# A selective scan fused with its decoder layer: the last chunk's production four pairs earlier, the out-projection in three pieces a tile

## The reference, cut to what matters

```python
xz = x @ W_in + b_in                                # 512 -> 2 x 1024
x_proj, z = jnp.split(xz, 2, axis=-1)
x_conv = silu(x_proj)                               # u
B, C = jnp.split(x_conv @ W_xproj + b_xproj, 2, axis=-1)        # 16 states each
dt = softplus(x_conv @ W_dt + b_dt)                 # 1024 -> 1024
# per token: h = h * exp(dt * A) + (dt * u) * B ; y = sum_s(h * C) + D * u
y = selective_scan(x_conv, dt, A, B, C, D_param)
y = y * silu(z)
x = layernorm(x + y @ W_out + b_out)
```

## Time and profile before

| | us |
|---|---|
| median of 3 runs | 3091.01 |
| lowest, highest | 3089.64, 3095.03 |
| the profiled execution | 3090.05 |
| its span | 3088.3 |
| scan phase: first scan, end of last scan | 57.2, 1916.9 |
| TensorE busy in the span | 2836.5 (92%) |
| VectorE busy | 2700.7 (87%) |
| ScalarE busy | 2008.9 (65%) |
| GpSimd busy | 1822.1 (59%) |

### The profile page before, as it was taken

One profiled execution on the slowest core, in us unless ns is written; L12 is line 12 of the kernel. 1 busy time (PEld: TensorE's weight loads), 2 busy tenths in 40 slices (PEclk: granted clock), 3 DMA queues, 4 the chain that ended last, 5 costly groups with the idle time before them and its releaser, 6 DMA issues. The chain is left out here.

```text
span 3088.3 us, 49028 instructions
## 1 busy us (share of the span) xinstructions
PE 2836.5 (92%) x18958; PEld 1265.0 (41%) x18958; DVE 2700.7 (87%) x3074; ACT 2008.9 (65%) x3598; POOL 1822.1 (59%) x936
## 2 busy tenths in 40 slices
PE   7988989889889889889899898999999999999998
PEld 2222222222222222222222223566666767667765
DVE  6999999999999999999999988776766777777775
ACT  6777777776776776776777644555555565655565
POOL 4887988988888888888988887312211111111100
PEclk9999999999999999999999999999999999999999
DMA  4112121111121121121112233701111000010000
GB/s 163 52 52 70 38 66 56 52 60 51 49 65 53 42 66 53 41 65 53 46 61 80 88 97 121 230 30 43 43 45 47 29 23 23 23 37 29 23 8 15
DMA packets 123897, 176.65 MB, mean 57 GB/s; under 512 B 15154, under 2 KB 50610, under 8 KB 123156
## 3 DMA queue, kind: packets, MB, share of 16 engines
q1 hardware_dynamic: 123668, 173.51, 17.4%
HBM read 104.33 MB, written 67.04 MB: 55 GB/s over the span
## 5 line engine op out<-in xcount | busy, mean ns | idle before, releaser
L900 POOL TENSOR_TENSOR h<-h,c_rep 128x1024 f32<-128x1024 f32 x511 | 1198.3, 2361 | 238.0 <-ACT carry L652 236.9
L796 DVE TENSOR_TENSOR_SCAN h<-r_ps,carry,h 128x512 f32<-128x512 f32 x768 | 949.2, 1289 | 3.6 <-ACT r_ps L646 3.6
L646 ACT ACTIVATE r_ps<-r_ps,decay 128x512 f32<-128x512 f32 x1024 | 632.7, 657 | 319.7 <-PE r_ps L397 318.9
L783 DVE TENSOR_TENSOR h<-u_ps,b_rep 128x1024 f32<-128x1024 f32 x512 | 625.8, 1222 | 10.8 <-PE u_ps L410 10.6
L410 PE MATMUL u_ps<-dtu,spread 32*128 32x512 f16 x2048 | 312.9, 383 | 117.3 <-DVE h L783 115.8
L397 PE MATMUL r_ps<-dt,spread 32*128 32x512 f16 x2048 | 313.1, 382 | 44.6 <-DVE h L796 44.4
L1979 POOL TENSOR_TENSOR o_in<-o_in,rows 128x1024 f32<-128x1024 f32 x15 | 37.0, 2469 | 489.0 <-DMA o_in<-o_dram 489.0
L796 DVE TENSOR_TENSOR_SCAN h<-r_ps,zero,h 128x512 f32<-128x512 f32 x256 | 315.1, 1278 | 7.1 <-ACT r_ps L646 7.0
L426 PE MATMUL y_ps<-h,gather 128*32 128x512 f32 x2048 | 284.8, 623 | 0.0
L40 PE MATMUL fps<-x,region 128*128 128x256 f16 x1024 | 280.3, 274 | 3.1 <-issue 2.4
L41 PE MATMUL fps<-x,region 128*128 128x256 f16 x1024 | 279.9, 273 | 0.0
(11 more groups left out here) (257 smaller groups left out, 5602.4 us busy)
## 6 DMA issues: line engine op xcount, KB each, us to landing
u_t_dram<-u SPq DMA_DIRECT2D x16, 1024.0 KB, 5.3
uz<-u_t_dram SPq DMA_DIRECT2D x64, 256.0 KB, 3.9
z_t_dram<-zs SPq DMA_DIRECT2D x32, 512.0 KB, 2.8
uz<-z_t_dram SPq DMA_DIRECT2D x64, 256.0 KB, 3.9
y_t_dram<-uz SPq DMA_DIRECT2D x64, 256.0 KB, 2.1
region<-y_t_dram SPq DMA_DIRECT2D x32, 256.0 KB, 3.5
result<-x SPq DMA_DIRECT2D x16, 512.0 KB, 2.8
x_t<-dram_x_t SPq DMA_DIRECT2D x15, 512.0 KB, 5.0
```

Of the source, the lines that this page charges most:

```text
L646: nc.scalar.activation(bank, bank, ACT.Exp, scale=decay[:, col:col + 1]).then_inc(s_da, 1)
L783: nc.vector.tensor_tensor(h[:, g % H_GROUPS, o:o + 2, :], u_ps[:, :, :], b_rep[:, c % 2:c % 2 + 1, :].broadcast_to([P, 2, TS]), ALU.mult). ...
L796: nc.vector.tensor_tensor_scan(row, r_ps[:, 2 * (pair % 2) + o, :], row, start, ALU.mult, ALU.add)\
L900: nc.gpsimd.tensor_tensor(rows, rows, c_rep[:, c % 2:c % 2 + 1, :].broadcast_to([P, 2, TS]), ALU.mult)\
```

## The change

The plan of chunk 7 starts at pair 22 of chunk 6 instead of 26, so that dt7 ends at s = 16 instead of 20; its x halves are converted at 15 and 20 instead of 19 and 23. Chunk 6's plan has no four-pair dt tiles any more (it ends at pair 20 of chunk 6 instead of 25). `w_out` is split from pair 11 (ScalarE) and 13 (VectorE). The out-projection starts at 19; first pieces stand at 19, 22, 25, 28, 31, 33, 36, 39, 42, 45, 47, 50, 53, 56, 59, 61; each tile has three pieces but tiles 4, 9, 14 and 15, which have two; the last piece is at 62. `x0_tile` runs a pair later, behind the scans of the pair after the tile's last. `keep_awake` covers two pairs (17, 18) instead of three. Some of SyncE's stores and loads in chunks 6 and 7 move up in its list.

```diff
-W_OUT_AT, OUT_AT = 15, 24
+W_OUT_AT, OUT_AT = 11, 19
...
-        start = {1: 32, 2: 27}.get(n, 26)
-        self.x = {1: (25, 28), 2: (21, 24)}.get(n, (19, 23))
+        start = {1: 32, 2: 27, NC - 1: 22}.get(n, 26)
+        self.x = {1: (25, 28), 2: (21, 24), NC - 1: (15, 20)}.get(n, (19, 23))
...
-            long = name in ("dt4", "dt5", "dt6", "dt7") and 2 <= n < NC - 1 or name == "dt3" and 3 <= n < NC - 1
+            long = name in ("dt4", "dt5", "dt6", "dt7") and 2 <= n < NC - 2 or name == "dt3" and 3 <= n < NC - 2
...
 class OutTile:
     def __init__(self, i):
-        at = OUT_AT + i // 2 * 5 + i % 2 * 3
-        self.pieces = {at + n: ks for n, ks in enumerate(((0, 4), (4, NJ)) if i % 2 else ((0, 3), (3, 6), (6, NJ)))}
+        at = OUT_AT + 3 * i - i // 5
+        self.pieces = {at + n: ks for n, ks in enumerate(((0, 4), (4, NJ)) if i % 5 == 4 or i == OUT_TILES - 1
+                                                         else ((0, 3), (3, 6), (6, NJ)))}
...
-                if j == 1:
+                if j == (1 if more else 0):
                     store_z(c, 2)
-                if j == 2:
+                if j == (2 if more else 1):
                     store_z(c, 3)
+                if j == 2 and c == NC - 2:
+                    next_x(c + 1, 1)
+                if j == 7 and c == NC - 2:
+                    store_z(c + 1, 1)
...
-                    if j == 2:
+                    if j == 2 and c < NC - 2:
                         next_x(c + 1, 1)
...
-                    if j == 7:
+                    if j == 7 and c < NC - 2:
                         store_z(c + 1, 1)
...
-                if s == OUTS[0].last:
+                if s == OUTS[0].last + 1:
                     x0_tile(0)
-                if s == OUTS[1].last:
+                if s == OUTS[1].last + 1:
                     x0_tile(1)
                     dve.wait_ge(s_oe, 2)
                     dve.sem_inc(a["s_x0"], 1)
```

## The result

| | before | after |
|---|---|---|
| median (20 runs of each) | 3093.45 | 3102.01 |
| lowest, highest | 3088.24, 3098.10 | 3096.43, 3104.77 |
| ratio, 95% interval | | 1.0027 [1.0021, 1.0033] |
| profiled execution | 3090.05 | 3100.17 |
| its span | 3088.3 | 3098.5 |

The account below looks back on a forecast made before the run. VectorE was taken to bound the scan phase. Terms -0.5 (chunk 6), 6.3 + 1.2 - 8.41 (out-projection's start), 2.9 + 0.8 - 5.17 (later pieces) and -2.0 (end) gave -4.9 from 3090.05: 3085.2, median 3085.5, range 3081 to 3089.5.

Parts of the forecast that it names:

- Part 1: Production four pairs sooner, chunk 6: VectorE covers the denser TensorE pairs; -0.5 us, idle of 1.22 could vanish or double.
- part 3: Out-projection's start in chunk 7: 6.3 us of waits plus 1.2 for the clock replace 8.41 idle.
- hold by tile 1's landing: Start of the out-projection: ScalarE held 5.3 us at y_high(1) by tile 1's late y, delaying exps(23); VectorE idles 3.6.
- Tile 1's pieces: Out-projection's start: pieces behind y_low(1, 0) and y_low(1, 1) cost VectorE 2.05 us, then two waits of 0.5 and 0.15.
- The clock: TensorE spells at the lower clock in chunk 7: 1.2 us added at the out-projection's start, 0.8 later; bounds 0 and 6.8.
- third rival: Long lower-clock spells after TensorE's waits at 19 and 21, up to 5.1 us each; say 3098, slower; chance 0.08.
- Part 4: Three pieces a tile, chunk 7 from pair 28: 2.9 us of late pieces plus 0.8 clock replace 5.17 idle.
- its four pairs: Chunk 7 pairs s = 31, 33, 47 and 61, said to pass 5.85 us and idle together 2.9.
- Part 5: End of the scan phase: last piece at 62 frees the carry, last gate sooner; gain 2.0 us, bounds 0 and 3.3.
- Part 2: w_out split from pair 11 in chunk 7: the same 7.5 us of VectorE work four pairs sooner, 0 change.
- second rival: Denser production makes TensorE late in 9-matmul pairs of chunks 5 to 7, giving back 3.8 us: 3089; chance 0.10.

Follow-up runs that it names:

- e3: Kernel after, with chunk 7's second x half converted at pair 19 instead of 20 and chunk 6's dt6 and dt7 splits later; 3092.36 us against before's 3091.61.
- e6: e3, with SyncE loading b_out, x and tile 1's y ahead of the weights and the wait for dt7; 3089.97 us, 0.9990 of before.
- e2: Kernel before, with only x0_tile a pair later; 3086.76 us against before's 3091.61.
- e10: e3, with the out-projection from pair 21, two-piece tiles where i % 3 == 2, and w_out split from pair 15; 3085.84 us against before's 3093.05.
- e11: e10, with w_out split from pair 11 instead of 15; 3086.69 us, 0.9978 of before.
- e8: Kernel before, with x0_tile a pair later, e6's loads first and chunk 7's dt6 and dt7 splits later; 3087.35 us against before's 3092.36.
- e5: e3, with chunk 7's dt6 and dt7 splits also moved later, to pairs 22 and 26; 3091.04 us, 0.9992 of before.
- e7: e3, with both e5's late splits and e6's loads first; 3094.36 us, 0.9993 of before.
- e12: e3, with the out-projection in its old places (15, 24) and x0_tile a pair later; 3093.31 us against before's 3093.05.

## Why the prediction was wrong

**Part 1 failed, and it carries the sign.** It looked at TensorE, pair by pair, and found cover: that was right (e3 keeps every matmul where it is and has no stop). The step that failed is "SyncE's moved stores and x load wait for conversions that also come four pairs sooner; I find none that holds back a load of u or z for a following tile: 0". It asked of the conversions only what the loads want of them. Nobody counted GpSimd, whose work of chunk 6's dt tiles (now denser) and of chunk 7's x (now sooner) falls into the same pairs: 30.4 us in 24.9, with the x half that u0's second piece waits for at their end. The term was -0.5; measured +9.0, outside its bounds of +-1.2. The row to read would have been GpSimd's busy time: 199.27 of 229.00 leaves 30 us in 64 pairs, half a us a pair.

**The start of the out-projection (part 3) failed by one missing waiter.** "TensorE waits 3.6 us" was worked out, and then priced only where `exps(23)` are late. Behind the waiting piece stand the sums of s = 19, and the gate of s = 20 waits for them. By the forecast's own numbers the piece starts at 11.1, its 9 matmuls take 2.0 and the sums 1.07, so the gate could start at 14.2, 1.3 later than the 12.9 (1755.53 - 1742.64) at which VectorE was free. To that come 2.4 (dt7 ended on GpSimd at 12.3 instead of 9.9, after TensorE's spell at the lower clock; in e3, without the long spell, it ended as foreseen) and 1.9 (the 9 matmuls and sums took 5.0 us at the lower clock, not 3.1). 1.3 + 2.4 + 1.9 = 5.6 of 5.66. The hold by tile 1's landing was 1.68 instead of 5.3, since the gate's stop hides the landing, and e6 shows that nothing is won without it. Tile 1's pieces cost 1.80 and 1.63 where 2.05 and 0.65 were foreseen. Together s = 16 to 26 idle 10.1, with the clock, against 7.5 foreseen and 8.41 before.

**The clock was undersized, the mechanism was there.** The first out piece and the first piece behind the stop in chunk 6 both run at the lower clock, as did 10.2 us from s = 14 on. Windows at these places, in order of time:

```profile
1527.50:1531.00 3.50, 3.47 (x10) 0.94 (x14) 0.00 (x0) 0.69 (x2) 2.27 (x1) 0.50 0.00 0
...
1733.01:1737.63 4.62, 4.49 (x13) 1.32 (x13) 4.62 (x6) 1.75 (x3) 4.54 (x3) 0.50 0.00 0
...
1756.10:1761.10 5.00, 4.94 (x21) 1.41 (x25) 0.00 (x0) 0.00 (x0) 5.00 (x4) 0.61 0.93 308
```

A matmul costs 0.43 there instead of 0.215; of the gate's 5.66 us this made 1.9. The Trainium skill (TensorE: Matmul & The Clock Gate, HAM oscillation — how this bites in real kernels) says that an idle gap sends the engine back to its lower clock and the next burst starts there; the first and third row agree, after waits of 7.41 and 5.81 us. The second does not show it: in the 10 us ahead of 1729.2, where that spell begins, TensorE's longest wait was 2.21. The third rival, that the clock alone makes the kernel slower, did not come true: chunk 7 is as long as before, and with the long spell gone (e3) it is only 3.2 us shorter.

**Part 4 came out by luck.** 3.64 us are idle from s = 28 on, where 3.7 were foreseen, but not as foreseen. The 3.7 were 2.9 of late pieces (its four pairs add up to 2.7) and 0.8 of clock; the 3.64 are late pieces at a full clock, 1.25 at s = 48 and 1.44 at s = 62 (47 and 61 were named), 0.60 and 0.20 at 32 and 34. And the 5.17 that they were set against held 1.7 of a spell at the lower clock, at s = 38, which the forecast had priced in "The clock" and did not take out. The old pieces at a full clock idle 3.30 from s = 30 on (e2): three pieces a tile won nothing. **Part 5 was right**: 1.57 won, 2.0 foreseen (the last section has a step that became longer). **Part 2** ("the same 7.5 us: 0") is right in the time (e10 against e11); the work itself became 6.7. `x0_tile`'s later place does what was said, and e2 shows what it wins alone: 6.0 us of idle, 4.3 without the spell at s = 38.

**The second rival** (denser production) has the right place and the wrong engine, at 3.8 us instead of 9.0. In sum: -0.5 became +9.0, -0.9 became +1.7, -1.5 stayed by luck, -2.0 became -1.6, and VectorE's own work in chunk 7 was 0.7 less: +6.9 against -4.9.

## What to carry to other kernels

- Where work is moved in hand-ordered queues, add up for every engine what the pairs around the new place hold, the engine that is nowhere critical too. A queue that is nearly full over the whole has no place for a bunch, and one small conversion at its end stops all others.
- When a piece must wait, list everything queued behind it on its engine and price each waiter; the nearest due one (here a gate) decides, not the one that the change was about.
- Before idle time of a trace is set down as what an order can win, take out what a spell at the lower clock made of it; a second trace of the same pieces shows it (here 2.02 against 0.33 us at one pair).
- Take a bundle apart. Here one part (`x0_tile` a pair later) won over 4 us of idle, one (the last piece at 62) 1.6, and two places (x half at 20, first piece at 19) lost 9 and gave back the rest. e10, with both places eased, is 8.0 us faster than before; whether it is faster than `x0_tile`'s two lines alone (4.3, 1.5 to 7.1) or e8 (6.2), the intervals leave open.

## What the runs showed of the hardware

Runs that hold the same code up to a point differ in whether TensorE falls to its lower clock there. Up to the end of chunk 6, e3, e5, e6, e7, e10, e11 and e12 run the same program. Windows of the same stretch, around pair 24 of chunk 6, first of e3, then of e6:

```profile
1522.00:1528.00 6.00, 6.00 (x23) 1.33 (x20) 6.00 (x6) 2.02 (x4) 5.92 (x4) 0.55 0.01 3
```

```profile
1522.00:1528.00 6.00, 5.98 (x37) 1.72 (x37) 6.00 (x7) 4.01 (x9) 5.92 (x5) 1.00 0.00 0
```

TensorE is busy throughout in both, with 23 matmuls in one and 37 in the other. Chunk 6 idles 3.26 to 3.30 in e3, e7, e10, e11 and e12, which have this spell, of 6.8 us from s = 22; 0.49 in e5, where a spell as long begins at s = 21; and 0.19 in e6, which has none. That is 3.1 us, as much as several edits of this study were worth. A place with such a spell should be costed from several executions, not from one, and the idle time of one trace is no measure to better than some 3 us. Whole executions scatter more: the first two chunks, whose code is the same in all fourteen kernels, took 465.2 to 472.1 us from the first scan.

`w_out_low` (L812) takes 1.19 to 1.24 us, or 2.08 to 2.23, or 3.0 to 3.1, over the kernels before, after, e10 and e11. Timeline of VectorE in the kernel after, two of the four:

```profile
1724.20 2.23 DVE L812 SCALAR_TENSOR_TENSOR region<-region 128x1024 f16<-128x1024 f32 x1
...
1739.99 1.19 DVE L812 SCALAR_TENSOR_TENSOR region<-region 128x1024 f16<-128x1024 f32 x1
```

and GpSimd's timeline beside them:

```profile
1722.98 2.37 POOL L905 TENSOR_TENSOR h<-h,c_rep 128x1024 f32<-128x1024 f32 x1 [1.48 <-ACT carry L657]
1725.31 2.14 POOL L892 TENSOR_TENSOR dt<-dt 128x512 f16<-128x512 f32 x1
1727.41 1.15 POOL L893 TENSOR_TENSOR dtu<-soft,dtu 128x512 f16<-128x512 f32 x1
```

At 1739.99 GpSimd falls idle (its weighing of 1737.66 ends at 1740.01), and the step takes 1.19. At 1724.20 it is weighing until 1725.35; the step ends 1.08 after that, and GpSimd's next step, 1.15 elsewhere, takes 2.14. Read so, the two engines exclude one another: VectorE waits for the rest of GpSimd's instruction, then GpSimd for VectorE's. One place of four steps costs VectorE 6.7 us (after, e11), another 8.6 (e10), before 7.5, and in e10 one of them, at 1750.16, makes `y_low(0, 0)` last 2.13. The scans and `dbu`, which have one input in PSUM (`r_ps`, `u_ps`), keep their 1.22 and 1.2 beside the weighings. The last multiplication by C (L863), both of whose inputs are in SBUF, took 3.37 beside a weighing of 2.35 that started 0.06 sooner, where it took 1.23 before: that is 2.1 us of the chain at the end. The Trainium skill (SBUF — State Buffer, SBUF: two separate sides) says that a VectorE operation with two SBUF inputs and a GpSimd operation that reads SBUF exclude each other for a whole instruction, and whichever starts first goes on; these rows agree.
